# Low halves of the next attention input: from VectorE to GpSimd

## The reference

```python
qkv = x @ Wqkv.T
q, k, v = jnp.split(qkv, 3, axis=-1)          # then 16 heads of 32
q = _phi(q); k = _phi(k)                      # elu(x) + 1
running_kv = _causal_decay_scan(k * v, decay, kv_init)
running_ksum = _causal_decay_scan(k, decay, ksum_init)
den = jnp.clip(jnp.sum(q * running_ksum, axis=-1, keepdims=True), 1e-06, None)
out = q * running_kv / den
...
g = jax.nn.sigmoid(out @ Wgate.T + bgate)
out = g * out + (1.0 - g) * v_direct
return out @ Wout.T
...
x = _layernorm(x + _L0_attn_ref(...), axis=-1)
x = _layernorm(x + _L0_xattn_ref(x, ctx_1024, ctx_1024), axis=-1)
x = _layernorm(x + _L0_ffn_ref(...), axis=-1)
```

## Time and profile before

| | us |
|---|---|
| median of 3 runs | 2797.39 (2795.37 to 2798.96) |
| the profiled execution | 2797.14 |
| its span, first to last instruction | 2795.4 |
| TensorE busy | 2600.7 (93%) |
| VectorE busy | 2009.5 (72%) |
| ScalarE busy | 1359.6 (49%) |
| GpSimd busy | 398.9 (14%) |
| mean granted clock of TensorE | 0.967 |

### The profile page before, as it was taken

One profiled execution on the slowest core, in us unless ns is written; L12 is line 12 of the kernel. 1 busy time (PEld: TensorE's weight loads), 2 busy tenths in 40 slices (PEclk: granted clock), 3 DMA queues, 4 the chain that ended last, 5 costly groups with the idle time before them and its releaser, 6 DMA issues.

```text
span 2795.4 us, 33065 instructions
## 1 busy us (share of the span) xinstructions
PE 2600.7 (93%) x11584; PEld 2180.7 (78%) x11584; DVE 2009.5 (72%) x2689; ACT 1359.6 (49%) x1698; POOL 398.9 (14%) x274
## 2 busy tenths in 40 slices
PE   2499999999999998299999999999999969999998
PEld 2378888888888887288888887888888758888886
DVE  8678888888888887344545446997777876666664
ACT  2235555555555555333333335888888822222222
POOL 3200000000000000000000001322222124333332
PEclk8699999999999999599999999999999989999999
DMA  6311111112111111444544535887677564444552
GB/s 240 143 46 61 60 68 60 60 65 98 69 60 68 60 60 46 174 164 151 166 157 159 172 125 204 288 292 263 247 264 254 203 267 196 195 195 203 208 223 109
DMA packets 146957, 429.20 MB, mean 154 GB/s; under 512 B 74848, under 2 KB 83296, under 8 KB 106592
## 3 DMA queue, kind: packets, MB, share of 16 engines
q1 hardware_dynamic: 143312, 402.43, 39.5%
q10 hardware_dynamic: 3600, 26.22, 2.3%
HBM read 234.62 MB, written 177.21 MB: 147 GB/s over the span
## 4 chain that ended last, share of the span: by engine, by line
PE 54%; DMA 1%; issue 1%; DVE 1%; ACT 1%; SPq 0%; POOL 0%; POOLq 0%; DVEq 0%; ACTq 0%
PE ff_ps L1727 12%; PE ff_ps L1728 12%; PE ff_ps L1729 12%; PE ff_ps L1764 6%; PE ff_ps L1765 6%; PE ff_ps L1766 6%; DMA ff_q<-x_ints 0%; DMA ff_gs<-gate_ints 0%; DMA ff_w_stage<-w_ffn_t 0%; DVE ff_sr L1649 0%; DMA up_products<-ff_group 0%; DVE ff_wl L1443 0%; ACT ff_group L1287 0%; DMA x_ints<-ff_up_abs 0%; ACT ff_group L1402 0%
## 5 line engine op out<-in xcount | busy, mean ns | idle before, releaser
L1727 PE MATMUL ff_ps<-ff_hi,ff_wh 128*128 128x512 f32 x1536 | 598.6, 390 | 49.7 <-DVE ff_lo L1449 46.5
L1728 PE MATMUL ff_ps<-ff_lo,ff_wh 128*128 128x512 f32 x1536 | 598.2, 389 | 0.0
L1729 PE MATMUL ff_ps<-ff_hi,ff_wl 128*128 128x512 f32 x1536 | 598.0, 389 | 0.0
L1287 ACT ACTIVATE ff_group<-ff_ps,ff_scales 128x512 f32<-128x512 f32 x384 | 257.6, 686 | 313.0 <-PE ff_ps L1729 302.3
L1727 PEld LDWEIGHTS ff_ps<-ff_hi,ff_wh 128*128 128x128 f32 x1536 | 288.8, 188 | 110.8 <-DVE ff_lo L1449 46.8
L1729 PEld LDWEIGHTS ff_ps<-ff_hi,ff_wl 128*128 128x128 f32 x1536 | 288.8, 188 | 60.0
L1728 PEld LDWEIGHTS ff_ps<-ff_lo,ff_wh 128*128 128x128 f32 x1536 | 288.8, 188 | 59.7
L1764 PE MATMUL ff_ps<-ff_wh,ff_hi 128*128 128x512 f32 x768 | 300.0, 391 | 24.2 <-DVE ff_lo L1665 23.5
L1765 PE MATMUL ff_ps<-ff_wl,ff_hi 128*128 128x512 f32 x768 | 299.7, 390 | 0.0
L1766 PE MATMUL ff_ps<-ff_wh,ff_lo 128*128 128x512 f32 x768 | 299.5, 390 | 0.0
L1460 DVE TENSOR_REDUCE ff_gate_max<-ff_group 128x2048 f32 (+1 forms) x48 | 109.7, 2286 | 217.1 <-ACT ff_group L1287 217.1
(11 more groups left out here) (192 smaller groups left out, 5149.0 us busy)
## 6 DMA issues: line engine op xcount, KB each, us to landing
gate_products<-ff_group SPq DMA_DIRECT2D x48, 1024.0 KB, 4.0
ff_raw<-gate_products SPq DMA_DIRECT2D x48, 1024.0 KB, 5.6
up_products<-ff_group SPq DMA_DIRECT2D x48, 1024.0 KB, 4.3
ff_raw<-up_products SPq DMA_DIRECT2D x48, 1024.0 KB, 9.3
gate_ints<-ff_gs SPq DMA_DIRECT2D x48, 512.0 KB, 2.6
ff_gs<-gate_ints SPq DMA_DIRECT2D x48, 512.0 KB, 9.9
xt_raw<-in_xT SPq DMA_DIRECT2D x64, 256.0 KB, 2.8
csq<-in_ctx_rows SPq DMA_DIRECT2D x16, 1024.0 KB, 6.8
```

Of the source, the lines that this page charges most:

```text
L1287: act.activation(group[:, g, m * T:(m + 1) * T], out_ps[(GM * g + m) % 6][:], ACT.Copy, scale=s_x).then_inc(evacuated, 1)
L1727: pe.matmul(o, wh[:, m, k], hi[:, par, k], start=(k == 0), stop=False)
L1728: pe.matmul(o, wh[:, m, k], lo[:, par, k], start=False, stop=False)
L1729: mm = pe.matmul(o, wl[:, m, k], hi[:, par, k], start=False, stop=(k == KC - 1))
```

## The change

VectorE no longer makes the low halves of the next sequence's input in steps 0 to 14; GpSimd makes all four of a step, each as soon as ScalarE's high half is there. The first sequence's input is still split by VectorE, ahead of step 0. GpSimd's stream is written anew in the same form as the others': in step s the root of the second norm with number s-1 (`due`), then the four subtractions, then the root of the first norm. The operands, the semaphores and what they count stay as they are.

```diff
--- before.py
+++ after.py
@@ -407,20 +407,33 @@
                 pool.affine_select(out=head_sum[:], in_=head_sum[:], compare_op=ALU.is_ge, fill=0.0,
                                    base=D - 1, pattern=[[-P, KC], [D, NH]], channel_multiplier=-1).then_inc(const_pool, 1)
 
+                def split_x(b, tiles):
+                    for k in tiles:
+                        pool.wait_ge(xh_ready, KC * b + k + 1)
+                        pool.tensor_tensor(xl[:, k], xt_raw[:, k % 2], xh[:, k].bitcast(F32),
+                                           ALU.subtract).then_inc(xl_ready, 1)
+
                 def root(n, s):
                     pool.wait_ge(ve_ready[n], s)
                     pool.tensor_tensor(rstd[n][:], var_eps[n][:], mhalf[:], ALU.pow).then_inc(rstd_ready[n], 1)
 
-                def step(s, front, back):
+                def step(s, back, nxt, due=True):
+                    if due:
+                        root(1, s - 1)
+                    if nxt:
+                        split_x(s + 1, range(KC))
                     if back:
                         root(0, s)
-                        root(1, s)
-
-                with pool.Fori(0, (NB - 2) // 2) as i:
+
+                step(0, False, True, False)
+                step(1, True, True, False)
+                with pool.Fori(1, (NB - 2) // 2) as i:
                     for u in range(2):
-                        step(2 * i + 1 + u, True, True)
-                step(NB - 1, True, True)
-                step(NB, False, True)
+                        step(2 * i + u, True, True)
+                step(NB - 2, True, True)
+                step(NB - 1, True, False)
+                step(NB, True, False)
+                root(1, NB)
                 pool.wait_ge(const_dve, 8)
                 pool.partition_all_reduce(dtmp2[:, 0:1], dtmp2[:, 0:1], P, bass.bass_isa.ReduceOp.max).then_inc(const_pool, 1)
 
@@ -555,6 +568,7 @@
                         dve.tensor_tensor(xl[:, k], xt_raw[:, k % 2], xh[:, k].bitcast(F32),
                                           ALU.subtract).then_inc(xl_ready, 1)
 
+
                 def front_phi(b, c):
                     n = KC * b + c
                     sl = c % 2
@@ -730,8 +744,6 @@
                     if front:
                         front_values(s, 3)
                         front_product(s, 3)
-                    if nxt:
-                        split_x(s + 1, (0, 1))
                     if front:
                         local_sums(s + 1, 1 - par)
                     if back:
@@ -740,8 +752,6 @@
                         reciprocals(s)
                     if back:
                         first_residual(s, 2)
-                    if nxt:
-                        split_x(s + 1, (2, 3))
                     if front:
                         last_sum_low(s + 1, 1 - par)
                     if back:
```

## The result

The changed kernel takes 2894.88 us (median of 4, 2892.59 to 2896.61) against 2798.18 us before (2795.37 to 2800.33): a ratio of 1.0346, 95% interval 1.0328 to 1.0364. It is slower, as forecast, but by 96.7 us and not by 27. The profiled execution has a span of 2890.9 us, 95.5 more than before. Two of all the runs behind this document, one of the kernel before (3432.79 us) and one of an experiment (4526.79), had a granted clock far lower than the others of the same kernel throughout, and no ratio uses them.

The account below looks back on a forecast made before the run. TensorE was taken to bound the attention stage, with `qks` of the fourth tile at zero slack. The median 2797.4 plus 15 steps x 1.8 us (27.0) gave 2824.4 us; range 2806 to 2836 us, its own 2820 to 2834.

Parts of the forecast that it names:

- GpSimd's first pair: `xl` 0 and 1, forecast to enter ahead of `kv` and `qks`: two holds, 1.8 us a step in 15 steps.
- VectorE's freed 2.6 us a step: Four subtractions fewer on VectorE in steps 0 to 14; costed at nothing, as TensorE has no idle time to give back.
- the race: Fourth tile's scan, `kv`, `qks` on VectorE against TensorE's denominators; slack 0.05 us, so any delay of `qks` goes through in full.
- The second pair: `xl` 2 and 3 on GpSimd, forecast done by 1033.0, TensorE asking at 1034.56: 1.5 us of cover, no cost.
- the size of a hold: Time GpSimd's 512-column subtraction keeps VectorE from its turn: taken as 0.90 us, range 0.84 to 1.12.
- The term: TensorE's waits for `qks` at the denominators: 15 steps x 1.8 us = 27.0 us.
- two reasons for the 6%: Against a falling clock: the wait is 1.8 us, not 3.2; steady steps have full matmuls between denominators, step 0 none.
- The rival: Each new wait at the denominators also lowers TensorE's clock: 14 steps x 2 = 28 us more, 2852 us; chance 6%.

Follow-up runs that it names:

- the kernel with a wait of 0.51 us: Kernel before, with one of VectorE's own subtractions for the next input moved ahead of the fourth `kv`, none on GpSimd: 2819.83 us, ratio 1.0079.
- The kernel with such a block and no wait: Kernel before, with all four groups of denominators ahead of the last product of the second projection group: 2821.15 us, 1.0084; same on the changed kernel: 2825.74 us, 1.0089.

## Why the prediction was wrong

**Right: where and how.** TensorE is the bound in the attention phase, and only `qks` of the fourth tile meets it without slack. GpSimd's first pair goes in at the end of the scan and between `kv` and `qks`, once each. VectorE's freed 2.6 us a step bring nothing (2799.43 us with all four subtractions on GpSimd and no hold in the race). The second pair is covered. Fifteen steps are hit and the sixteenth is not: from the root at 1133.61 to the last at 1195.06 the step is 61.45 us. The feed-forward phase did not change.

**Off by a little: the size of a hold.** I took 0.90 us of 0.84 to 1.12, by quarters of the 2048-column rows; measured are 1.05 and 1.06 on VectorE. The term came out as 30.4 us and not 27.0. The two subtractions of GpSimd in the race take 3.47 us together with the waits in them, 1.7 each and not 1.4 to 1.6. A quarter was the wrong reading: the rows of the two widths fit an instruction with a part that doesn't shrink with its columns. The trace of the kernel with only the second pair on GpSimd has the length with hardly anyone in the way (count, then least, median and longest ns):

```profile
L414 POOL TENSOR_TENSOR xl<-xt_raw,xh x30: 1261/1296/1745, 166.9 to 1032.6; 128x512 fp32r<-128x512 f32 x30
```

1.26 us at least for 512 columns, 3.64 for 2048: (3.64 - 1.26) / 1536 = 1.55 ns a column and 0.47 us that are always there, an estimate from two widths and two operations. The figure of the Trainium skill for 2048 columns (GPSIMD Engine Reference, Elementwise — side-by-side cycle accounting), which I had turned into an estimate of 1.12 us for 512, was the nearer one to the hold of 1.05, by luck: it is a quarter too, of a longer time.

**Wrong: the clock was left out of the sum.** This is the step that failed. The forecast prices TensorE's wait at its own length and keeps the clock at 1.00; that the clock falls too stood among the rivals with 6%. In the changed kernel it fell in each of the thirteen steps measured, and all that the waits leave over, 65 of the 95.5 us, goes with it. I gave two reasons for the 6%, and the runs refute both. *The wait is 1.8 us and not the 3.2 of step 0*: waits of 0.51 us do it in every fourth step, 1.11 in every second, 2.0 in each. *Full matmuls stand between the denominators*: they are worth something, since a block without them makes the clock fall by itself, but behind a wait they didn't prevent it; the kernel with a wait of 0.51 us has them too. I had taken a single case, step 0, for the price of a wait and for a threshold. Its rows show two causes at once, 3.2 us of waiting and then a block of 32 small matmuls, in which the clock falls:

```profile
161.51 5.90 PE L841 MATMUL qk_ps<-head_sum,qks 128*128 128x16 f32 x32 [3.19 <-DVE qks L574]
...
160.00:162.00 2.00, 0.49 (x5) 0.49 (x5) 2.00 (x4) 0.00 (x0) 0.00 (x0) 1.00 0.00 0
162.00:164.00 2.00, 2.00 (x15) 2.00 (x15) 1.97 (x4) 0.00 (x0) 0.00 (x0) 0.69 0.00 0
```

So they say neither that 3.2 us of wait are needed nor that they are enough. The kernel with such a block and no wait shows that the block is.

**The price of it was too small as well.** I put 2 us a step, from the 4 us at half rate behind the resumed full matmuls of step 0. In step 7 the fall comes within 2.7 us of the end of the wait and the clock stays at 0.50 for 10 us (501 to 511), of which the 16-column matmuls are part: 4.85 us a step. The rival's 2852 us would have been wrong by 43.

The sum by what was measured, for the steps 1 to 14: waits 28.3 us (14 x 2.02), half clock 14 x 4.85 = 68; with 2 more for step 0 that is 98 against 96.6 at the roots (thirteen steps are measured; that step 1 had the same is assumed).

The Trainium skill has a related case (TensorE: Matmul & The Clock Gate, A second HAM failure mode: psum-queue depth-cycling): in a kernel of 512-column bf16 matmuls, very short idle spells between groups of matmuls were frequent enough to make the clock go back and forth between its two levels. The trace of the changed kernel agrees with it: one short wait a step, and 10 us at 0.50 behind it in step 7. The rival deserved more than 6%.

## What to carry to other kernels

Before work is handed to GpSimd, look at what VectorE does at the moment when it will start: here two of its two-input instructions were held for 1.05 us each, so a subtraction of 0.65 us that was taken off VectorE cost it more than it freed. In a kernel whose TensorE never waits, a new wait of TensorE must be priced with the clock: here waits of 0.5 and of 2.0 us a step both cost about three times their length (22 us for 7.7, 97 for 30.4). What mended it here was to move TensorE's request behind other full matmuls (nine of them) and to keep the small matmuls spread among full ones.

## What the runs showed of the hardware

- **Falls of the clock come in a share of the steps, not by a threshold.** Waits of 0.51, 1.11, 1.45 and 2.02 us gave 3, 6, 9 and 13 falls in 13 steps, at regular intervals, each worth 4.4 to 5.9 us. Each of these waits had groups of small matmuls behind it.
- **Small matmuls in a row bring the clock down too.** 32 of 16 columns, with no wait at all, brought it to 0.50 for some 3 us in the step shown: 0.8 to 0.9% of the kernel, on two kernels.
- **A GpSimd subtraction of 128x512** takes 1.26 us at least (median 1.30 where it stood out of the race) and held a two-input instruction of VectorE for 1.05 us.
